# Four style-modulated convolution layers folded into one nine-tap convolution per sample: fifteen products of 512 columns, or twenty-four of 256 on even and odd columns

## The chip, the cores and the metric

The kernel runs on one core of one Trainium2 chip. The metric is device time in microseconds (us), the median of the runs shown; lower is better. The core's engines run side by side, each through its own list of instructions in the order written, and meet only at semaphores: TensorE (PE in the views; its weight loads are PEld), VectorE (DVE), ScalarE (ACT), GpSimd (POOL), and the queue engine SyncE (SP), which starts most of the DMA transfers.

## What is computed

128 samples of 64 channels and 1024 positions go through four 1D convolution layers with three taps each. The weights of a layer are scaled per sample by a style vector and normalised, and the input is added at the end:

```python
TYPES = ('same', 'upsample', 'same', 'downsample')
s = style @ mw.T + mb
weight = SCALE * w * s[:, None, :, None]
demod = lax.rsqrt(jnp.sum(weight * weight, axis=(2, 3)) + EPS)
weight = weight * demod[:, :, None, None]
# 'same': conv + bias; 'upsample': transposed conv, then blur [1,3,3,1];
# 'downsample': blur [1,3,3,1], then conv of stride 2
...
x = x + layers(x, cond_512)
```

Nothing nonlinear lies between the layers, so for one sample the chain is one convolution of nine taps, but for the outermost positions, which the kernel computes apart ("edges").

## The kernel before

**Layout.** A sample is 128 rows (two parities of the position times 64 channels) by 512 columns. In this form nine taps are five matrices of 128x128, one for each shift of a column. They are called W, and each sample has its own five.

**Groups and pairs.** Work goes by groups of NG = 4 samples (32 groups, for which weights are built) and by pairs of Q = 2 samples (loads, stores, splits of x). All in the program is float32, fed to TensorE as two parts of type fp32r: a high part (`xh`, `Wh`, made on ACT by a cast) and a low part (`xl`, `Wl`, the difference, made on DVE or POOL). A product is three matmuls, high by high, low by high, high by low (`split_mm`, L156 to L159).

**The main convolution** (`conv`) of a sample is five products with 512 columns, 15 matmuls, into one PSUM bank `po`. ACT then scales it, adds a bias and writes it to `T` (`t_out`, L398); POOL puts the edge values in (`finish`), and SP stores.

**The weights of a group** come out of seven units of TensorE, u0 to u6, each of which writes `pg`, one of three PSUM banks in rotation. Between them the results pass DVE (scaled by numbers per sample, `full`), ACT (high part, `high`) and POOL (low part, `low`):
- u0, u1 (10 matmuls): last two layers, result `Q2f`, high part `Q2h`, low parts `Q2l` and, for a lone half, `Q2h` written in place by POOL (L166).
- u2, u3 (24 matmuls) read Q2, result `Gf`, then `Gh`, `Gl`.
- u4, u5, u6 (22 matmuls) read G, result `Wf`; `ID`, made on POOL, adds the residual. `Wh` on ACT, `Wl` on DVE (`w_low`).
- `Q3f`, `Q3h`, `Q3l` feed u0 and u1, and are made three groups ahead.

Those are 56 matmuls of 256 columns for a group. SP then copies half of W across the partitions (`cross`, eight DMAs), since each matrix needs the blocks of two column shifts.

**The order** is written out by hand. Every engine loops over the samples b; i = b mod 4 is the slot in the group, and `SLOTS[i]` says which units, of how many groups ahead, TensorE runs ahead of conv(b), and the other engines go by the same table. In front of the loop a prologue makes the constants and the first weights.

```python
SLOTS = [[(1, 4), (2, 0), (2, 1)], [(1, 5), (1, 6)], [(2, 2)], [(2, 3)]]
for b in range(B):                       # TensorE
    for x in units_of(b):
        unit(*x)
    conv(b)
```

On DVE an iteration is: `x_low` for the pair after next (even b), then `full` for the slot's units, then `w_low` (slots 0 and 1), then a step of the edges (in four slots of group 0 and in slot 3 of groups 3 to 6, 11 to 14 and 19 to 22). On POOL it is: `ID` (slot 0), `low` of the slot's units, Q3 work (slots 2 and 3), `finish` (odd b).

Of the kernel before, what the change touches and what calls it, by code (L numbers as in the profile page):

```python
# [41 lines left out]
def build(nc, xin, xe, cw, a2, b1, q3, ed, wt, mwt, bb, st, eye, out):  # L42
    with ExitStack() as ctx:
# [96 lines left out]
        s_a2 = sem("a2l")  # L140
        s_pp, s_ch, s_one, s_ms, s_sq, s_sc, s_k0, s_b1 = (
            sem(n) for n in ("pp", "ch", "one", "ms", "sq", "sc", "k0", "b1"))


        SC_SQ2, SC_A2, SC_SQ, SC_A, SC_D, SC_K1, SC_K2, SC_K3, SC_CV = range(1, 10)

        K_A2, K_C, K_B1, K_B1D = 1, 2, 4, 8
# [41 lines left out]
        def _(sp):  # L189
            for n, dst, src in (("mwt", MW[:], mwt.rearrange("p (l m) -> p l m", l=4)),  # L190
                                ("bb", BB[:], bb.rearrange("p (k l) -> p k l", k=2)),
                                ("b1", b1w, b1),
                                ("q3", q3s[:], q3.rearrange("p (k o) -> p k o", k=2)),
                                ("eye", EYE[:], eye)):
# [49 lines left out]
        def _(pe):  # L244
            def conv(b):
                g, i = divmod(b, NG)
                n, q = divmod(b, Q)
# [4 lines left out]
                if q == 0:
                    pe.wait_ge(s_xh, n + 1)
                    pe.wait_ge(s_xl, n + 1)
                if b >= 2:
# [595 lines left out]
```

## Time and profile before

| | |
|---|---|
| median of 3 runs | 759.41 us (758.45 to 761.19) |
| the profiled execution | 762.67 us |
| its span, first to last instruction | 760.7 us |
| busy in the span: PE, DVE, ACT, POOL | 92%, 46%, 39%, 38% |
| TensorE's granted clock, mean | 0.984 |

Busy time adds up what an engine spent in instructions. A timeline row gives start, duration, engine, line of the kernel, operation, out<-in with shapes; brackets hold the idle time ahead of it and who ended it. The start-to-start distance of two matmuls is their real cost, since matmuls overlap. A windows row gives busy time of each engine in a stretch, then TensorE's granted clock, in which 1.00 is 2.4 GHz and 0.50 is 1.2 GHz.

### The profile page before, as it was taken

What the parts mean: (1) busy time and instruction counts of PE and PEld (TensorE: products, weight loads), DVE (VectorE), ACT (ScalarE), POOL (GpSimd) and SP (SyncE); (2) the same over time, 40 slices, a digit from 0 to 9 for tenths busy, and PEclk for the clock granted to TensorE, in tenths of its full rate; (3) what the DMA queues carried; (4) which work ended last, traced back from release to release, by engine and by line L of the source; (5) the groups of instructions that cost most, each with busy time, mean ns of one, the idle gap of its engine ahead of it and who ended that gap; (6) DMA issues with size and microseconds to landing.
All of it is one profiled execution on the core that took longest, in us unless ns stands there. A gap on an engine that the chain in (4) does not pass through costs nothing.

```text
span 760.7 us, 10551 instructions
## 1 busy us (share of the span) xinstructions
PE 702.8 (92%) x3830; PEld 608.2 (80%) x3830; DVE 348.7 (46%) x551; ACT 298.6 (39%) x435; POOL 289.3 (38%) x437
## 2 busy tenths in 40 slices
PE   2256989999999999999999999999999999999997
PEld 1245878888788888888888888888888888888886
DVE  5666663343555343443654433434654334334430
ACT  2222234444344444434344344443443444444432
POOL 5353134434333444334234444343334443433310
PEclk9986999999999999999999999999999999999999
DMA  7022455666766666666757766767657667667752
GB/s 251 0 42 77 92 138 124 152 162 131 161 156 159 161 144 147 157 148 145 168 144 155 162 143 155 151 144 170 154 134 168 147 152 156 144 161 174 174 145 84
DMA packets 187939, 109.00 MB, mean 143 GB/s; under 512 B 154032, under 2 KB 154288, under 8 KB 187888
## 3 DMA queue, kind: packets, MB, share of 16 engines
q1 hardware_dynamic: 187232, 106.56, 60.0%
q10 hardware_dynamic: 656, 1.77, 0.8%
q8 instruction: 31, 0.51, 0.3%
q14 instruction: 20, 0.16, 0.1%
HBM read 37.00 MB, written 33.55 MB: 93 GB/s over the span
## 4 chain that ended last, share of the span: by engine, by line
PE 73%; DVE 9%; POOL 8%; issue 6%; ACT 2%; DMA 1%; POOLq 0%; ACTq 0%; DVEq 0%
PE po L157 15%; PE po L158 15%; PE po L159 15%; PE pg L157 7%; PE pg L159 6%; PE pg L158 6%; PE pg L163 3%; PE pg L162 3%; DVE Gf L614 2%; POOL Q3h L166 2%; POOL Q3l L510 2%; POOL Gh L166 2%; POOL Gl L529 2%; ACT Gh L418 1%; DMA T<-in_wt 1%
## 5 line engine op out<-in xcount | busy, mean ns | idle before, releaser
L157 PE MATMUL po<-xh,Wh 128*128 128x512 f32 x640 | 253.5, 396 | 0.0
L159 PE MATMUL po<-xh,Wl 128*128 128x512 f32 x640 | 253.1, 396 | 0.0
L158 PE MATMUL po<-xl,Wh 128*128 128x512 f32 x640 | 253.0, 395 | 0.0
L398 ACT ACTIVATE T<-po,cv,DD 128x512 f32<-128x512 f32 x128 | 99.7, 779 | 155.7 <-PE po L159 155.5
L595 DVE TENSOR_TENSOR xl<-X,xh 128x1032 fp32r<-128x1032 f32 x64 | 81.8, 1278 | 142.8 <-ACT xh L391 142.6
L159 PEld LDWEIGHTS po<-xh,Wl 128*128 128x128 f32 x640 | 120.9, 189 | 28.2
L158 PEld LDWEIGHTS po<-xl,Wh 128*128 128x128 f32 x640 | 121.6, 190 | 23.3
L157 PEld LDWEIGHTS po<-xh,Wh 128*128 128x128 f32 x640 | 121.5, 190 | 23.1
L526 POOL TENSOR_TENSOR Gl<-Gf,Gh 128x512 fp32r<-128x512 f32 x32 | 41.5, 1297 | 231.4 <-ACT Gh L418 231.3
L423 ACT CAST Wh<-Wf 128x512 fp32r<-128x512 f32 x64 | 46.6, 727 | 153.9 <-DVE Wf L618 92.8
L518 POOL TENSOR_TENSOR Q2l<-Q2f,Q2h 128x512 fp32r<-128x512 f32 x32 | 44.1, 1377 | 121.4 <-ACT Q2h L413 121.4
L418 ACT CAST Gh<-Gf 128x512 fp32r<-128x512 f32 x64 | 39.7, 620 | 116.1 <-DVE Gf L614 116.1
L614 DVE TENSOR_TENSOR Gf<-pg,D10c 128x512 f32<-128x512 f32 x64 | 44.0, 688 | 85.3 <-PE pg L163 85.3
L391 ACT CAST xh<-X 128x1032 fp32r<-128x1032 f32 x64 | 66.7, 1042 | 6.6 <-DVE cv L769 6.6
L618 DVE TENSOR_TENSOR Wf<-pg,S 128x512 f32<-128x512 f32 x64 | 43.9, 686 | 53.5 <-PE pg L163 53.0
L630 DVE TENSOR_TENSOR Wl<-Wf,Wh 128x512 fp32r<-128x512 f32 x64 | 52.5, 820 | 30.2 <-ACT Wh L423 30.2
L157 PE MATMUL pg<-Q2h,B1h 128*128 128x256 f32 x192 | 56.3, 293 | 4.8 <-DVE B1dl L727 4.8
L157 PE MATMUL pg<-Gh,Ch 128*128 128x256 f32 x192 | 57.4, 299 | 3.0 <-DVE Wf L618 3.0
L159 PE MATMUL pg<-Q2h,B1l 128*128 128x256 f32 x192 | 55.8, 291 | 0.0
L158 PE MATMUL pg<-Q2l,B1h 128*128 128x256 f32 x192 | 55.7, 290 | 0.0
L159 PE MATMUL pg<-Gh,Cl 128*128 128x256 f32 x192 | 54.8, 285 | 0.0
L158 PE MATMUL pg<-Gl,Ch 128*128 128x256 f32 x192 | 54.7, 285 | 0.0
(155 smaller groups left out, 999.0 us busy)
## 6 DMA issues: line engine op xcount, KB each, us to landing
X<-in_xin SPq DMA_DIRECT2D x64, 516.0 KB, 5.9
out<-T SPq DMA_DIRECT2D x64, 512.0 KB, 3.6
Wh<-Wh SPq DMA_DIRECT2D x96, 128.0 KB, 2.9
Wl<-Wl SPq DMA_DIRECT2D x96, 128.0 KB, 3.2
Wh<-Wh SPq DMA_DIRECT2D x32, 192.0 KB, 4.9
Wl<-Wl SPq DMA_DIRECT2D x32, 192.0 KB, 5.3
E<-in_ed ACTq DMA_DIRECT2D x1, 768.0 KB, 9.8
XE<-in_xe SPq DMA_DIRECT2D x1, 576.0 KB, 11.8
```

What stands on the lines that cost most here:

```text
L157: eng.matmul(o, wh_, rh, start=first, stop=False)
L158: eng.matmul(o, wh_, rl, start=False, stop=False)
L159: return eng.matmul(o, wl_, rh, start=False, stop=last)
L391: act.copy(xh[:, n % XH], X[:, n % XR]).then_inc(s_xh, 1)
L398: act.activation(T[:, n % TR, b % Q], po[b % 2][:, :], ACT.Identity, bias=cv[:, b:b + 1], scale=DD[:, 3, b:b + 1]).then_inc(s_t, 1)
L418: act.copy(Gh[:, v], Gf[:, v]).then_inc(s_gh, 1)
L423: act.copy(wv(Wh, g, v), wv(Wf, g, v)).then_inc(s_wh, 1)
L518: pool.tensor_tensor(Q2l[:], Q2f[:, 0:2], r32(Q2h[:, 0:2]), ALU.subtract).then_inc(s_q2l, 1)
L595: tt(xl[:, n % XH], X[:, n % XR], r32(xh[:, n % XH]), ALU.subtract).then_inc(s_xl, 1)
L614: m = tt(v4(Gf[:, 2 * u - 4:2 * u - 2]), two, bc2(gs(D10c, g), 2, C), ALU.mult)
L618: m = tt(v4(Wf[:, 2 * u - 8:2 * u - 6]), two, bc2(gs(S[:, 0], g), 2, C), ALU.mult)
L630: tt(wv(Wl, g, v), wv(Wf, g, v), r32(wv(Wh, g, v)), ALU.subtract).then_inc(s_wl, 1)
```

## The change

The convolution of a sample is rewritten on even and odd columns. With W0 to W4 the five matrices, e the even and o the odd columns of x, both results share one sum: M[k] = (W0+W1) o[k] + (W2+W3) o[k+1] + W4 o[k+2]. The even result is M plus W0, W2, W4 applied to e-o, the odd one is M plus W1, W3 applied to the shifted e minus o. These are 3+3+2 products of 256 columns where five of 512 stood, so 24 matmuls of 256 columns, not 15 of 512.

For this
- POOL makes the two differences for each pair (`x_parts`, two operations of 128x516), in place in `X`; the row of `X`, `xh` and `xl` grows from 1032 to 1548 elements for a pair; the ring of `xh` and `xl` shrinks from three to two, that of `X` from four to three. `x_high` and `x_low` go one pair ahead, not two.
- POOL makes W0+W1, W2+W3 and W1+W2 (`sums`, 128x512 and 128x256), ACT and DVE their high and low parts (`sums_high`, `sums_low`).
- M has PSUM banks of its own (`pm`). ACT scales it and adds the bias (`m_out`, 128x256), and DVE adds it to both halves of `po` and writes `T` (`t_out`, 128x512, now on DVE, in front of the next sample's units).
- The weights lie with the four samples innermost, in one tensor `W`; a weight load of the convolution reads 128 columns that are 16 bytes apart. `cross` is five DMAs with runs of 256 elements, not 64.
- The slots change: u4, u5, u6 stand together in slot 0, u0 and u1 in slot 1.
- In the prologue DVE takes the low parts of group 0 and the running sums of `b1s` from POOL.

```diff
-SLOTS = [[(1, 4), (2, 0), (2, 1)], [(1, 5), (1, 6)], [(2, 2)], [(2, 3)]]
+SLOTS = [[(1, 4), (1, 5), (1, 6)], [(2, 0), (2, 1)], [(2, 2)], [(2, 3)]]
...
@@ TensorE, conv(b)
-                for j in range(5):
-                    w = [t[:, g % 2, j * NG + i].rearrange("p r o -> p (r o)") for t in (Wh, Wl)]
-                    m = split_mm(pe, po[b % 2][:, :], w[0], w[1], xh[:, n % XH, q, j:j + L2], xl[:, n % XH, q, j:j + L2],
-                                 j == 0, j == 4)
-                m.then_inc(s_o, 1)
+                def part(o, blocks, x):
+                    for j, v in enumerate(blocks):
+                        w = [W[:, g % 2, v, t].rearrange("p r (o b) -> p (r o) b", b=NG)[:, :, i] for t in range(2)]
+                        m = split_mm(pe, o, w[0], w[1], *[t[:, n % XH, q, x + j:x + j + 256] for t in (xh, xl)],
+                                     j == 0, j == len(blocks) - 1)
+                    return m
+                if b >= 2:
+                    pe.wait_ge(s_m, b - 1)
+                part(pm[b % 2], (5, 6, 4), HW).then_inc(s_mm, 1)
+                if b >= 2:
+                    pe.wait_ge(s_t, b - 1)
+                part(po[b % 2][:, 0:256], (0, 2, 4), 0)
+                part(po[b % 2][:, 256:512], (1, 3), 2 * HW).then_inc(s_o, 1)
...
@@ ACT
-            def t_out(b):
...
+            def m_out(b):
+                act.wait_ge(s_mm, b + 1)
+                if b >= 2:
+                    act.wait_ge(s_t, b - 1)
+                act.activation(M[:, b % 2, :], pm[b % 2], ACT.Identity,
+                               bias=cv[:, b:b + 1], scale=DD[:, 3, b:b + 1]).then_inc(s_m, 1)
+            def sums_high(g):
+                act.wait_ge(s_ws, 2 * g + 1)
+                act.copy(W[:, g % 2, 5:7, 0, 0], Wf[:, 5:7]).then_inc(s_wh, 1)
+                act.wait_ge(s_ws, 2 * g + 2)
...
+                act.copy(Wx[:, 0], Wf[:, 7]).then_inc(s_wh, 1)
...
@@ POOL
+            def x_parts(n):
+                pool.wait_ge(s_x[n % XR], 16 * (n // XR + 1))
+                x = X[:, n % XR]
+                pool.tensor_tensor(x[:, :, 2 * HW:3 * HW], x[:, :, 1:HW + 1], x[:, :, HW:2 * HW], ALU.subtract
+                                   ).then_inc(s_ab, 1)
+                pool.wait_ge(s_ab, 2 * n + 1)
+                pool.tensor_tensor(x[:, :, 0:HW], x[:, :, 0:HW], x[:, :, HW:2 * HW], ALU.subtract).then_inc(s_ab, 1)
...
+            def sums(g):
+                pool.wait_ge(s_ce, cnt(g, 5))
...
+                pool.tensor_tensor(Wf[:, 5:7], Wf[:, 0:4:2], Wf[:, 1:4:2], ALU.add).then_inc(s_ws, 1)
+                pool.tensor_tensor(Wf[:, 7], Wf[:, 1], Wf[:, 2], ALU.add).then_inc(s_ws, 1)
...
             for b in range(B):
                 g, i = divmod(b, NG)
                 if i == 0 and g + 1 < NGR:
                     identity(g + 1)
+                    sums(g + 1)
                 for x in units_of(b):
                     if x[1] < 4:
                         low(*x)
+                if b % Q == 0 and b and b // Q + 2 < NQ:
+                    x_parts(b // Q + 2)
...
@@ DVE
+            def t_out(b):
+                n, q = divmod(b, Q)
+                dve.wait_ge(s_m, b + 1)
+                dve.wait_ge(s_o, b + 1)
...
+                dve.scalar_tensor_tensor(out=T[:, n % TR, q].rearrange("p (e k) -> p e k", e=2),
+                                         in0=po[b % 2][:, :].rearrange("p (e k) -> p e k", e=2),
+                                         scalar=DD[:, 3, b:b + 1],
+                                         in1=M[:, b % 2, :].unsqueeze(1).to_broadcast([128, 2, 256]),
+                                         op0=ALU.mult, op1=ALU.add).then_inc(s_t, 1)
...
             for b in range(B):
                 g, i = divmod(b, NG)
-                if b % Q == 0 and b // Q + 2 < NQ:
-                    x_low(b // Q + 2)
+                if b:
+                    t_out(b - 1)
                 for x in units_of(b):
                     full(*x)
+                if b % Q == 0 and b and b // Q + 1 < NQ:
+                    x_low(b // Q + 1)
                 if i == 0 and g + 1 < NGR:
                     w_low(g + 1, 0)
-                if i == 1 and g + 1 < NGR:
                     w_low(g + 1, 1)
+                    sums_low(g + 1)
```

DVE in the main loop, from slot 0 of a group to its slot 2, before. `xl` is `x_low`, `Wf` are u4 to u6, `Q2f` u0 and u1, `Wl` `w_low`, `Gf` u2 or u3:

```order
L595 TENSOR_TENSOR xl<-X,xh 128x1032
L618 TENSOR_TENSOR Wf<-pg,S 128x512
L607 TENSOR_TENSOR Q2f<-pg,D 128x512
L609 TENSOR_TENSOR Q2f<-pg,D 128x256
L630 TENSOR_TENSOR Wl<-Wf,Wh 128x8x64
L618 TENSOR_TENSOR Wf<-pg,S 128x512
L622 TENSOR_TENSOR Wf<-Wf,ID 64x256
L624 TENSOR_TENSOR Wf<-pg,S 128x256
L630 TENSOR_TENSOR Wl<-Wf,Wh 128x12x64
L595 TENSOR_TENSOR xl<-X,xh 128x1032
```

The same engine and place after; here `W` and `Wx` are `w_low` and `sums_low`, and `T<-po,DD,M` is `t_out`:

```order
L665 TENSOR_TENSOR Wf<-pg,S 128x512 x2
L669 TENSOR_TENSOR Wf<-Wf,ID 64x256
L671 TENSOR_TENSOR Wf<-pg,S 128x256
L629 TENSOR_TENSOR xl<-X,xh 128x1548
L677 TENSOR_TENSOR W<-Wf,W 128x2x256
L677 TENSOR_TENSOR W<-Wf,W 128x3x256
L681 TENSOR_TENSOR W<-Wf,W 128x2x256
L683 TENSOR_TENSOR Wx<-Wf,Wx 64x256
L637 SCALAR_TENSOR_TENSOR T<-po,DD,M 128x512
L653 TENSOR_TENSOR Q2f<-pg,D 128x512
L655 TENSOR_TENSOR Q2f<-pg,D 128x256
```

The two operations on `Q2f` have moved from in front of all of the work on W to behind the whole of it, and five operations of two SBUF inputs now stand in a row between `Wf` and `t_out`.

POOL from slot 0 of a group to slot 1, before (`T<-EP` is `finish`):

```order
L537 TENSOR_TENSOR ID<-EYE,inv 128x256
L518 TENSOR_TENSOR Q2l<-Q2f,Q2h 128x512
L166 TENSOR_TENSOR Q2h<-Q2f,Q2h 64x256
L544 COPY T<-EP 128x2x2
L545 COPY T<-EP 128x2x2
```

The same engine and place after (`Wf<-Wf` is `sums`, `X<-X` `x_parts`):

```order
L558 TENSOR_TENSOR ID<-EYE,inv 128x256
L566 TENSOR_TENSOR Wf<-Wf 128x512
L567 TENSOR_TENSOR Wf<-Wf 128x256
L518 TENSOR_TENSOR X<-X 128x2x258
L521 TENSOR_TENSOR X<-X 128x2x258
L539 TENSOR_TENSOR Q2l<-Q2f,Q2h 128x512
L177 TENSOR_TENSOR Q2h<-Q2f,Q2h 64x256
```

`sums` and `x_parts` have come in between `ID` and the low parts of Q2.

## Rows read from the trace of the kernel before

**Rows 1.** The page: busy time, share of the span, instructions

```profile
PE 702.8 (92%) x3830; PEld 608.2 (80%) x3830; DVE 348.7 (46%) x551; ACT 298.6 (39%) x435; POOL 289.3 (38%) x437
```

**Rows 2.** Windows: stretch, length, busy PE, PEld, DVE, ACT, POOL, clock, DMA

```profile
145.52:255.05 109.53, 108.28 (x605) 94.01 (x605) 53.10 (x87) 45.40 (x66) 43.10 (x66) 1.00 0.67 151
642.71:663.81 21.10, 20.88 (x117) 18.05 (x117) 8.45 (x12) 9.12 (x14) 8.51 (x14) 1.00 0.70 157
```

**Rows 3.** Timeline of TensorE, steady: start, duration, line, operation

```profile
652.50 0.28 PE L157 MATMUL pg<-Q2h,B1h 128*128 128x256 f32 x1
...
654.05 0.28 PE L163 MATMUL pg<-Q2h,B1dl 128*128 128x256 f32 x1
654.17 0.39 PE L157 MATMUL po<-xh,Wh 128*128 128x512 f32 x1
...
654.87 0.39 PE L157 MATMUL po<-xh,Wh 128*128 128x512 f32 x1
```

**Rows 4.** Groups of VectorE by shape: busy us, mean ns, idle before

```profile
L595 DVE TENSOR_TENSOR xl<-X,xh 128x1032 fp32r<-128x1032 f32 x64 | 81.8, 1278 | 142.8 <-ACT xh L391 142.6
L630 DVE TENSOR_TENSOR Wl<-Wf,Wh 128x768 fp32r<-128x768 f32 x32 | 30.7, 958 | 28.8 <-ACT Wh L423 28.8
L630 DVE TENSOR_TENSOR Wl<-Wf,Wh 128x512 fp32r<-128x512 f32 x32 | 21.8, 681 | 1.4 <-ACT Wh L423 1.4
```

**Rows 5.** Groups of ScalarE by shape, same columns

```profile
L398 ACT ACTIVATE T<-po,cv,DD 128x512 f32<-128x512 f32 x128 | 99.7, 779 | 155.7 <-PE po L159 155.5
L418 ACT CAST Gh<-Gf 128x512 fp32r<-128x512 f32 x64 | 39.7, 620 | 116.1 <-DVE Gf L614 116.1
```

**Rows 6.** Groups of GpSimd by shape, same columns

```profile
L526 POOL TENSOR_TENSOR Gl<-Gf,Gh 128x512 fp32r<-128x512 f32 x32 | 41.5, 1297 | 231.4 <-ACT Gh L418 231.3
L505 POOL TENSOR_TENSOR Q3f<-q3s,D 128x512 f32<-128x512 f32 x31 | 32.6, 1051 | 0.2
L529 POOL TENSOR_TENSOR Gl<-Gf,Gh 128x256 fp32r<-128x256 f32 x32 | 23.7, 740 | 37.5 <-ACT Gh L418 37.5
```

**Rows 7.** Timeline of VectorE and of GpSimd where the two overlap

```profile
47.20 1.63 DVE L595 TENSOR_TENSOR xl<-X,xh 128x1032 fp32r<-128x1032 f32 x1
...
50.12 0.69 DVE L630 TENSOR_TENSOR Wl<-Wf,Wh 128x512 fp32r<-128x512 f32 x1 [0.69 <-ACT Wh L423]
50.73 0.68 DVE L618 TENSOR_TENSOR Wf<-pg,S 128x512 f32<-128x512 f32 x1
51.45 0.42 DVE L622 TENSOR_TENSOR Wf<-Wf,ID 64x256 f32<-64x256 f32 x1
51.79 0.41 DVE L624 TENSOR_TENSOR Wf<-pg,S 128x256 f32<-128x256 f32 x1
...
47.13 0.61 POOL L537 TENSOR_TENSOR ID<-EYE,inv 128x256 f32<-128x256 f32 x1
47.70 2.29 POOL L518 TENSOR_TENSOR Q2l<-Q2f,Q2h 128x512 fp32r<-128x512 f32 x1
50.14 1.26 POOL L166 TENSOR_TENSOR Q2h<-Q2f,Q2h 64x256 fp32r<-64x256 f32 x1
```

**Rows 8.** Windows of TensorE: stretch, length, busy PE, clock, DMA

```profile
40.70:44.35 3.65, 0.09 (x2) 1.00 0.00 0
44.35:47.90 3.55, 3.55 (x17) 0.53 0.00 0
...
99.10:101.79 2.69, 0.22 (x2) 1.00 0.00 0
...
102.60:105.90 3.30, 3.30 (x12) 0.50 0.48 158
```

**Rows 9.** Timeline of TensorE: first unit, first convolution, a unit in group 1's slot 0

```profile
28.00 0.55 PE L157 MATMUL pg<-Q3h,A2h 128*128 128x256 f32 x1 [8.70 <-POOL Q3h L166]
...
73.71 0.63 PE L157 MATMUL po<-xh,Wh 128*128 128x512 f32 x1
...
101.79 0.35 PE L157 MATMUL pg<-Q3h,A2h 128*128 128x256 f32 x1 [2.47 <-POOL Q3h L166]
```

More of the change, by code:

```diff
@@ L139, in build @@
         s_e, s_ed = sem("e"), sem("ed")
[L140 to L147, printed above, removed]
+        s_a2, s_cl = sem("a2l"), sem("cl")
+        s_pp, s_ch, s_one, s_ms, s_sq, s_sc, s_k0, s_b1, s_bs = (
+            sem(n) for n in ("pp", "ch", "one", "ms", "sq", "sc", "k0", "b1", "bs"))
+        SC_SQ2, SC_A2, SC_SQ, SC_D32, SC_A, SC_D, SC_K1, SC_K2, SC_K3, SC_CV = range(1, 11)
+        K_A2, K_C, K_B1, K_B1D = 1, 2, 3, 4
         r32 = lambda ap: ap.bitcast(F32)
@@ L345, in _ @@
             for l in range(4):
-                m = pe.matmul(ps[:, l * 128:l * 128 + 128], MW[:, l, :], ST[:, :], start=True, stop=True)
+                m = pe.matmul(ps[:, l * 128:l * 128 + 128], MW[:, l, :], ST, start=True, stop=True)
             m.then_inc(s_pp, 1)
@@ L427, in _ @@
             act.wait_ge(s_in["wt"], 16)
+            act.activation(SQ[:, 2], WT[:, 2], ACT.Square).then_inc(s_sq, 1)
             act.activation(SQ[:, 0:2], WT[:, 0:2], ACT.Square)
@@ L472, in _ @@
                         high(*x)
+                m_out(b)
+                if i == 0 and g + 1 < NGR:
+                    sums_high(g + 1)
                 if i == 3 and g + 3 < NGR:
                     q3_high(g + 3)
-            t_out(B - 1)
         @block.gpsimd
@@ L558, in _ @@
             low(1, 1)
+            sums(0)
             q3_full(2)
@@ L562, in _ @@
             low(1, 3)
+            x_parts(1)
+            x_parts(2)
             for b in range(B):
@@ L719, in _ @@
             reached(dve.tensor_scalar(AA[:, 3], psv[:, 3], EPS, None, ALU.add))
+            dve.wait_ge(s_k0, K_B1)
+            tt(B1l[:, :, 0, :], b1s[:, 0:11:2, :], r32(B1h[:, :, 0, :]), ALU.subtract)
+            tt(B1l[:, :, 1, :], b1s[:, 2:13:2, :], r32(B1h[:, :, 1, :]), ALU.subtract).then_inc(s_b1, 1)
             full(0, 0)
@@ L734, in _ @@
             full(0, 2)
+            full(0, 3)
+            dve.wait_ge(s_gh, 1)
+            tt(Gl[:, 0:2], Gf[:, 0:2], r32(Gh[:, 0:2]), ALU.subtract).then_inc(s_gl, 1)
+            dve.wait_ge(s_gh, 2)
+            tt(Gl[:, 2], Gf[:, 2], r32(Gh[:, 2]), ALU.subtract).then_inc(s_gl, 1)
+            lone_low(dve, Gh[hi, 3, :], Gf[hi, 3, :]).then_inc(s_gl, 1)
+            link(dve.reciprocal(RR[:, 3], RR[:, 3]))
             newton(slice(3, 4))
             reached(tt(inv3[:], AA[:, 3], DD[:, 3], ALU.mult))
-            full(0, 3)
             full(1, 0)
             full(1, 1)
-            x_low(0)
             full(0, 4)
-            w_low(0, 0)
             full(0, 5)
             full(0, 6)
+            w_low(0, 0)
             w_low(0, 1)
+            x_low(0)
+            sums_low(0)
             dve.wait_ge(s_in["ed"], 16)
@@ L787, in _ @@
                         edge_in(c + 1)
+            t_out(B - 1)
 def layouts(x, cond_512, w, bia, mw, mb):
```

298 lines of the change are left out of this document (156 added, 142 removed).

## The prediction, made before the changed kernel ran

> **What bounds the kernel now.** I read the page first: TensorE is busy 92% of the span, no other engine half of it [rows 1]. Then the windows: one group of four samples takes 21.10 us [rows 2]. The timeline gives the price of a matmul in it as the distance of two starts: 13 distances of 256 columns take 1.55 us, 0.119 each; three of 512 take 0.70 us, 0.233 each [rows 3]. So 56 unit matmuls (6.7) and 60 convolution matmuls (14.0) are 20.7 us; 0.4 us of the 21.1 is waiting. TensorE is the bound, and the other engines have slack: DVE 8.45 busy in 21.10, POOL 8.51 [rows 2].
>
> **What TensorE saves.** 96 matmuls of 256 columns at 0.119 are 11.4 us where 60 of 512 took 14.0. TensorE's work in a group falls to 18.1 us. Were it still the bound, 31 groups would give back some 90 us. I argue that it isn't: the change puts work and order on DVE and POOL that close a longer loop.
>
> **Durations of what is new.** For each the nearest row, ends behind it.
> - `x_low`, 1548 elements: the undelayed 1032 take 1.23 (1.63 less a delay worked out below [rows 7]) and 512 take 0.68 [rows 4]. That is 1.06 ns for an element, so 1.78 us (1.7 to 1.9).
> - `t_out` on DVE: as another 512 out of PSUM, 0.68 [rows 7]; up to 0.78, which ACT took [rows 5]. `w_low` 0.68 and 0.96 [rows 4], `sums_low` 0.68 and 0.42 [rows 4, 7].
> - `m_out` on ACT, 256: 0.40 to 0.78, taken 0.56; it frees ACT and lies beside other work [rows 5].
> - POOL: `x_parts` 1.30 twice a pair (1.05 to 1.40), `sums` 1.30 and 0.74 [rows 6]. POOL gets 7.2 us a group on top of its 8.5, DVE 4.9 on top of its 8.45 (`t_out` 2.7, `xl` 1.1, `sums_low` 1.1).
> - Series on DVE step by duration less 0.08: 50.73, then 51.45 behind a semaphore, 51.79 [rows 7].
>
> **Two inputs in SBUF on DVE and a read on POOL don't run together.** At 47.13 POOL's `ID` starts (0.61, ends 47.74); `xl` starts at 47.20 and ends 48.83; `Q2l` on POOL starts at 47.70 and ends 49.99, for 2.29 instead of 1.3. Each time the second ends at the first one's end plus its own duration less 0.15: 47.74+1.23-0.15 = 48.82; 48.83+1.30-0.15 = 49.98. It holds for `Wl` and `Q2h` too: 50.81+0.74-0.15 = 51.40, the row's 50.14+1.26. `Wf` out of PSUM, begun at 50.73 beside the same `Q2h`, took its plain 0.68, so one SBUF input doesn't collide, and `t_out` won't [rows 7]. The Trainium skill, "SBUF — State Buffer", section "Who interferes with whom", has the same collision, but as a lock for the whole instruction. By it each of the seven turns below would cost 0.15 us more, a group 1.1 us; the rows' 0.15 of overlap stands in my sum.
>
> **The new loop, u2 of one group to u2 of the next.** Before, u0 and u1 ran in slot 0 and u2 in slot 2, two convolutions later. Now u0 and u1 are in slot 1, and between them and u2 stands one convolution (24 x 0.119 = 2.9 us), while DVE does all work on W ahead of `full` of u0. First with no collision and no idle engine:
> - TensorE from u2 to the end of u5: u2 14, conv 24, u3 10, conv 24, u4 9, u5 11, which is 92 matmuls, 10.95 us, and 0.2 until DVE sees it.
> - DVE: u5 0.68, `ID` added 0.50, u6 0.35, `x_low` 1.70, `w_low` 0.60 and 0.88, `sums_low` 0.60 and 0.35, `t_out` 0.60, `full` of u0 0.68: 6.9 us.
> - ACT 0.65, POOL 1.30 for `Q2l`, 0.08, 0.74 for the lone half, 0.1 to TensorE: 2.9 us.
>
> That is 21.0 us, more than TensorE's 18.1 and no less than the group of before. The loop alone eats the gain.
>
> Now with POOL's turns, t = 0 at u2's start. TensorE has waited before u2, so I take its clock as low at first: after 2.7 and 3.65 us of idle it ran at 0.50 for some 3.4 us, 0.21 for a matmul of 256 [rows 8]. u2 ends at 3.0, its Gf at 3.9, Gh at 4.55. DVE goes on with `x_low` from 3.8 to 5.6, so POOL's `Gl` ends at 6.75, `x_parts` at 9.4, `Q3f` at 10.4. u3's low halves, ready to start at 9.5, run 10.45 to 11.95. u4 ended at about 12.0, so u5 starts at 12.05 and ends 13.35. POOL: two Q3 halves 13.55, `finish` 13.9, `ID` 14.5. DVE adds `ID` by 14.95. From there both engines take turns, each with the step above: `sums` a to 16.3, `x_low` 17.9, `sums` b 18.5, `w_low` a 19.05, `x_parts` a 20.2, `w_low` b 21.0, `x_parts` b 22.15, `sums_low` a 22.7, b 23.05. `t_out` 23.65, `full` of u0 24.25, Q2h 24.9, Q2l 26.25, lone half 27.05, u2 at **27.1 us**. TensorE ended the convolution of slot 1 at 20.5 and idles 6.6 us.
>
> **The sum.** Before the first convolution DVE makes u0's Q3 parts at once, not behind 2 us of `B1l` on POOL; I take 67 us for 73.7 (65 to 74). Group 0, with four steps of the edges, was 28.1 us [rows 9]; it was 7 over a plain group, and I take 10 over the new one, 37. Groups 1 to 29 have a u2 ahead: 29 x 27.1 = 786. In groups with an edge step DVE was busy (53.10 - 5 x 8.45)/4 = 2.7 us more each, and the group grew by only (109.53 - 5 x 21.10)/4 = 1.0 [rows 2]. In the new loop DVE's step comes ahead of u5's `full` after a wait for TensorE: 3.3 each, 12 x 3.3 = 40. The last two groups have no u2: 16 (their W chain) and 12; the tail 4. 67+37+786+40+16+12+4 = 962 us of span. The profiled execution is 2 over its span and 3 over the median, so I say **960 us**, 26% slower. Cross copies (fewer, longer runs) and the rings of two and three cost nothing: W is ready some 9 us before its convolution, and `xh` frees a slot early.
>
> **The rivals.**
> 1. *The same turns, but the clock stays high.* u2 then ends 1.3 us earlier and so does POOL's chain: 25.8 a group, 38 less: 920.
> 2. *The turns cost little* (DVE and POOL slip into each other's gaps, or `x_parts` reads in another way). The loop of 21.0 with POOL's u3 halves is 21.3, with the clock low after a wait of 3 us 22.6. 67+34+29x21.3+30+28+4 = 781, up to 818: 800. Against it: the steps of [rows 7] fit to 0.01 us.
> 3. *Strided weight loads.* No row has a weight load with columns 16 bytes apart. Below, it costs nothing; above, the step of 0.119 hides at least a whole load now [rows 3], and a load of twice that would make a convolution matmul 0.238. The loop holds 48 of them, 5.7 us, of which 1 hides behind POOL: 29 x 4.7 = 136, so 1096. The Trainium skill, "SBUF — State Buffer", the note on cachelines, says that each access to a new line of 16 bytes pays a penalty, and that two hits in a line are needed for full bandwidth; that would bring this rival, though the same note calls a stride of 4 fp32 free. By the first reading 1096, by the second 960.
> 4. *TensorE remains the bound* (the other side). The loop must then lose 3 us more than the rows allow, say by DVE's subtractions on the new layout going at twice the speed, or by waits of u2 that I place wrongly. Then 67 + 28 + 29 x 18.4 + 30 + 4 + 12 = 675. It decides at a loop of 18.1, and faster than before begins at one of about 20.
> 5. *A loop of 20 to 20.5*: no change.
>
> **Chances.** Forecast 0.43, rival 1 0.15, rival 2 0.14, rival 3 0.13, rival 4 0.12, rival 5 0.03. Forecast and rivals 1 to 3 are 0.85, so the range reaches from 775 to 1110; the forecast's own is 900 to 1010. A measurement of this kernel tells 0.3% from no change: faster 0.12, same 0.03, slower 0.85.
>
> **What would show it.** A group of 27 us in the windows, with TensorE idle in one piece before u2 (`Q2h, B1h`), released by POOL's lone half of Q2; TensorE some 67% busy; its clock at 0.50 after that idle time; POOL's `sums` and `x_parts` and DVE's `xl` and `W` stretched far over their plain durations, in turns; DVE's stretch from u5 to `t_out` 8 us long. Wrong, if u2 follows the convolution of slot 1 at once, if those durations stay plain (rival 2), if the matmuls on `W` step by more than 0.13 in warm stretches (rival 3), or if the first convolution is not before 74 us.

## The result, and the profile after

The changed kernel takes **1092.79 us** (1091.89 to 1093.98), the kernel before 759.45 (758.45 to 761.19): 1.439 times as long, interval 1.4357 to 1.4417. That is inside the forecast's wide range, but 133 us over its value, and within 3 us of what the third rival gave (1096).

The page of after, as [rows 1] for before, and two of its groups (busy us, mean ns, idle before):

```profile
PE 988.9 (91%) x4982; PEld 979.1 (90%) x4982; DVE 561.3 (51%) x755; ACT 334.3 (31%) x498; POOL 607.7 (56%) x615
...
L566 POOL TENSOR_TENSOR Wf<-Wf 128x512 f32<-128x512 f32 x32 | 140.2, 4381 | 145.3 <-DVE Wf L669 145.3
...
L168 PEld LDWEIGHTS po<-xh,W 128*128 128x128 f32 x640 | 211.8, 331 | 0.0
```

TensorE is as busy as before, 91%, though its matmuls go over fewer columns in all. The windows, columns as in [rows 2], show one plain group:

```profile
611.38:641.86 30.48, 29.39 (x152) 29.23 (x152) 15.09 (x19) 10.28 (x16) 19.14 (x20) 1.00 0.49 126
```

A group is 30.48 us, not 21.10, at the full clock, and TensorE fills 29.39 of it with 152 matmuls. The timeline of TensorE at the end of slot 1, as [rows 3], tells why:

```profile
639.35 0.40 PE L170 MATMUL po<-xh,W 128*128 128x256 f32 x1
...
640.75 0.39 PE L170 MATMUL po<-xh,W 128*128 128x256 f32 x1
642.23 0.35 PE L168 MATMUL pg<-Q2h,B1h 128*128 128x256 f32 x1 [1.08 <-POOL Q2h L177]
642.42 0.28 PE L169 MATMUL pg<-Q2l,B1h 128*128 128x256 f32 x1
642.54 0.28 PE L170 MATMUL pg<-Q2h,B1l 128*128 128x256 f32 x1
642.65 0.28 PE L168 MATMUL pg<-Q2h,B1h 128*128 128x256 f32 x1
```

Six distances of the convolution's 256 columns take 1.40 us, 0.233 each, as much as 512 columns took [rows 3]; those of a unit take 0.12 as ever. So 96 x 0.2335 + 56 x 0.119 = 29.1, and some 1.3 us of waiting ahead of u2 make the group. The convolution costs 22.4 us a group where the old one cost 14.0.

Behind that the forecast's loop is there too. DVE and GpSimd from u5's `Wf` to u2's low parts:

```profile
629.24 0.42 DVE L669 TENSOR_TENSOR Wf<-Wf,ID 64x256 f32<-64x256 f32 x1
629.58 0.41 DVE L671 TENSOR_TENSOR Wf<-pg,S 128x256 f32<-128x256 f32 x1
629.91 1.75 DVE L629 TENSOR_TENSOR xl<-X,xh 128x1548 fp32r<-128x1548 f32 x1
631.59 1.54 DVE L677 TENSOR_TENSOR W<-Wf,W 128x512 fp32r<-128x512 f32 x2
634.96 1.62 DVE L681 TENSOR_TENSOR W<-Wf,W 128x512 fp32r<-128x512 f32 x1 [1.82 <-ACT W L441]
636.61 1.21 DVE L683 TENSOR_TENSOR Wx<-Wf,Wx 64x256 fp32r<-64x256 f32 x1
637.85 0.75 DVE L637 SCALAR_TENSOR_TENSOR T<-po,DD,M 128x512 f32<-128x512 f32 x1
...
629.73 4.54 POOL L566 TENSOR_TENSOR Wf<-Wf 128x512 f32<-128x512 f32 x1 [3.42 <-DVE Wf L669]
634.23 0.74 POOL L567 TENSOR_TENSOR Wf<-Wf 128x256 f32<-128x256 f32 x1
634.94 1.10 POOL L518 TENSOR_TENSOR X<-X 128x516 f32<-128x516 f32 x1
636.11 1.43 POOL L521 TENSOR_TENSOR X<-X 128x516 f32<-128x516 f32 x1
639.93 1.28 POOL L539 TENSOR_TENSOR Q2l<-Q2f,Q2h 128x512 fp32r<-128x512 f32 x1 [2.39 <-ACT Q2h L427]
641.35 0.73 POOL L177 TENSOR_TENSOR Q2h<-Q2f,Q2h 64x256 fp32r<-64x256 f32 x1
```

From the start of DVE's `ID` operation (629.24) to u2 (642.23) it takes 13.0 us, where the prediction had 12.6 (14.5 to 27.1). TensorE is busy with the slow convolution through nearly all of it and idle for 1.1 us.

### The profile page after: what moved, and what is told of

The parts are those of the page before. It is cut to its first block, busy times and chain, and to the rows that moved or that the text cites. A ratio compares the mean times of both kernels' runs of the same rounds, so it can differ in the third digit from the quotient of the medians.

```text
span 1090.6 us, 13458 instructions
## 1 busy us (share of the span) xinstructions
PE 988.9 (91%) x4982; PEld 979.1 (90%) x4982; DVE 561.3 (51%) x755; ACT 334.3 (31%) x498; POOL 607.7 (56%) x615
## 4 chain that ended last, share of the span: by engine, by line
PE 49%; POOL 19%; DVE 19%; issue 8%; ACT 4%; DVEq 0%; DMA 0%; POOLq 0%; SPq 0%
POOL Wf L566 13%; PE po L168 7%; PE po L170 7%; PE po L169 7%; PE pg L168 5%; PE pm L169 4%; PE pm L170 4%; PE pm L168 4%; PE pg L170 4%; PE pg L169 4%; POOL Q2l L539 3%; DVE Wx L683 3%; DVE T L637 3%; DVE Wf L665 3%; POOL Q2h L177 2%
## 5 line engine op out<-in xcount | busy, mean ns | idle before, releaser
L168 PE MATMUL po<-xh,W 128*128 128x256 f32 x640 | 254.7, 398 | 0.0
L169 PE MATMUL po<-xl,W 128*128 128x256 f32 x640 | 254.7, 398 | 0.0
L170 PE MATMUL po<-xh,W 128*128 128x256 f32 x640 | 254.1, 397 | 0.0
L566 POOL TENSOR_TENSOR Wf<-Wf 128x512 f32<-128x512 f32 x32 | 140.2, 4381 | 145.3 <-DVE Wf L669 145.3
L169 PEld LDWEIGHTS po<-xl,W 128*128 128x128 f32 x640 | 211.9, 331 | 0.0
L168 PEld LDWEIGHTS po<-xh,W 128*128 128x128 f32 x640 | 211.8, 331 | 0.0
L170 PEld LDWEIGHTS po<-xh,W 128*128 128x128 f32 x640 | 211.7, 331 | 0.0
L169 PE MATMUL pm<-xl,W 128*128 128x256 f32 x384 | 153.5, 400 | 0.0
L170 PE MATMUL pm<-xh,W 128*128 128x256 f32 x384 | 153.4, 399 | 0.0
L168 PE MATMUL pm<-xh,W 128*128 128x256 f32 x384 | 152.4, 397 | 0.0
L169 PEld LDWEIGHTS pm<-xl,W 128*128 128x128 f32 x384 | 127.0, 331 | 0.0
L170 PEld LDWEIGHTS pm<-xh,W 128*128 128x128 f32 x384 | 126.9, 331 | 0.0
L168 PEld LDWEIGHTS pm<-xh,W 128*128 128x128 f32 x384 | 124.7, 325 | 0.0
L629 DVE TENSOR_TENSOR xl<-X,xh 128x1548 fp32r<-128x1548 f32 x64 | 113.5, 1774 | 6.1 <-ACT xh L406 6.1
```

What stands on the lines that cost most here:

```text
L168: eng.matmul(o, wh_, rh, start=first, stop=False)
L169: eng.matmul(o, wh_, rl, start=False, stop=False)
L170: return eng.matmul(o, wl_, rh, start=False, stop=last)
L566: pool.tensor_tensor(Wf[:, 5:7], Wf[:, 0:4:2], Wf[:, 1:4:2], ALU.add).then_inc(s_ws, 1)
L629: tt(xl[:, n % XH], X[:, n % XR], r32(xh[:, n % XH]), ALU.subtract).then_inc(s_xl, 1)
```

## The experiments

Theory: the weight load's stride sets the convolution's step (the distance of two starts), and without it the prediction's walk through a group holds. Rival: something else in the 256-column products, or in the reads of x, makes them slow.

**c1: neighbouring weights.** Only the address of the convolution's weight loads differs; the products then use the wrong columns of `W`.

```diff
-w = [W[:, g % 2, v, t].rearrange("p r (o b) -> p (r o) b", b=NG)[:, :, i] for t in range(2)]
+w = [W[:, g % 2, v, t].rearrange("p r n -> p (r n)")[:, 128 * i:128 * i + 128] for t in range(2)]
```

> The changed kernel with one thing different: a weight load of the convolution reads 128 neighbouring elements and not 128 that are 16 bytes apart. It therefore multiplies by wrong weights; all else, every instruction and wait, is as in the changed kernel. Theory L (the strided load sets the step of the convolution's matmuls, 0.2335 us in the changed kernel): the step falls to 0.119, TensorE's own work in a group falls from 29.1 to 18.1 us, and the group of 30.5 us becomes the loop through DVE and POOL that the prediction works out, 26 to 27.1 us with a low clock after the idle time: 950 to 990 us in all. If that loop is weaker than worked out: group 21.5 to 24, 800 to 880 us. Rival M (the step comes from something else in the new matmuls, such as the shifted moving columns or the PSUM halves): step stays 0.2335, 1093 us. Rival of a TensorE that is the bound again: group 18.4, 675 us.

Measured 974.6 us (974.07 to 975.5), ratio 1.2824 (1.2795 to 1.2853). Windows of a group, of TensorE's wait and of the stretch behind it, and TensorE's timeline at the end of the wait:

```profile
605.14:632.52 27.38, 20.80 (x152) 20.63 (x152) 15.11 (x18) 10.04 (x16) 19.09 (x20) 0.87 0.55 140
625.85:632.52 6.67, 0.45 (x4) 0.24 (x2) 5.03 (x6) 2.85 (x5) 4.05 (x4) 0.91 0.00 0
632.52:635.90 3.38, 3.03 (x14) 3.06 (x15) 0.00 (x0) 0.13 (x1) 0.52 (x3) 0.50 0.56 187
...
632.87 0.55 PE L168 MATMUL pg<-Q2h,B1h 128*128 128x256 f32 x1 [6.57 <-POOL Q2h L177]
```

The step is 0.119 us, and this is the kernel that the prediction described: a group of 27.34 us (27.1 foretold), TensorE idle for 6.6 us ahead of u2 behind GpSimd's lone half of Q2 (6.6 foretold), then 3.4 us at half the clock, and 974.6 in all (960). The load's addresses alone make the 118 us between c1 and after.

**c2, c3, b4: which stride.** c2 takes every second column of `W` (8 bytes apart), c3 every third (12), again wrong ones; b4 is the kernel before with its loads 16 bytes apart.

```diff
c2 +...rearrange("p r n -> p (r n)")[:, 64 * i:64 * i + 256:2]
c3 +...rearrange("p r n -> p (r n)")[:, 32 * i:32 * i + 382:3]
b4 -w = [t[:, g % 2, j * NG + i].rearrange("p r o -> p (r o)") for t in (Wh, Wl)]
b4 +w = [t[:, g % 2, j * NG:(j + 1) * NG].rearrange("p n r o -> p (n r o)")[:, i:512:4] for t in (Wh, Wl)]
```

> As c1_contiguous, but the weight load's elements are 8 bytes apart (wrong weights again). If a load costs more only from 16 bytes on, or as soon as two elements share a line of 16 bytes it is free: step 0.119 and the time of c1_contiguous within 1%. If the cost grows with the distance: load between 190 and 331 ns, step about 0.16 to 0.18, group 27 to 29.

> As c1_contiguous, with elements 12 bytes apart (wrong weights again), so that three of four elements open a new line of 16 bytes. If the limit is a distance of 16 bytes: as c1_contiguous. If each new line costs: the step is near 0.2, time near that of the changed kernel, 1050 to 1093 us.

> The kernel before with one thing different: the weight load of the 512-column matmuls reads 128 elements 16 bytes apart (wrong weights). Theory L with a load that runs beside the matmul ahead (step is the longer of the two): the load needs 0.2335, the matmul 0.233, so the step and the 759 us stay within 1%, and the load's duration rises from 190 to 331 ns. If load and matmul share the time in part (0.233 plus the extra 0.115), the step is 0.35, a group 21.1 + 60 x 0.115 = 28.0 and the time 970 to 985 us. If strides cost nothing (rival M): 759 us and loads of 190 ns.

Measured c2 975.05, c3 1028.17 (one run each), b4 780.12 us (779.82 to 781.1; ratio 1.0263, 1.0236 to 1.029). c2 came out as its first case. c3 lies between its two cases, and b4 above the 1% of its theory. The weight loads of the first product in the groups by shape, of c1, c2, c3 (mean 196, 202, 264 ns; 331 in after, above), then of before and of b4:

```profile
L168 PEld LDWEIGHTS po<-xh,W 128*128 128x128 f32 x640 | 125.5, 196 | 3.3 <-DVE T L637 3.3
```

```profile
L168 PEld LDWEIGHTS po<-xh,W 128*128 128x128 f32 x640 | 129.1, 202 | 3.3 <-DVE T L637 3.3
```

```profile
L168 PEld LDWEIGHTS po<-xh,W 128*128 128x128 f32 x640 | 169.2, 264 | 0.2 <-DVE T L637 0.2
```

```profile
L157 PEld LDWEIGHTS po<-xh,Wh 128*128 128x128 f32 x640 | 121.5, 190 | 23.1
```

```profile
L157 PEld LDWEIGHTS po<-xh,Wh 128*128 128x128 f32 x640 | 198.6, 310 | 0.2
```

TensorE's timelines at the full clock, of c2, c3 and then b4:

```profile
597.58 0.28 PE L168 MATMUL po<-xh,W 128*128 128x256 f32 x1
...
599.16 0.28 PE L169 MATMUL po<-xl,W 128*128 128x256 f32 x1
```

```profile
600.05 0.34 PE L168 MATMUL po<-xh,W 128*128 128x256 f32 x1
...
600.91 0.34 PE L170 MATMUL po<-xh,W 128*128 128x256 f32 x1
```

```profile
599.93 0.40 PE L158 MATMUL po<-xl,Wh 128*128 128x512 f32 x1
...
601.60 0.40 PE L159 MATMUL po<-xh,Wl 128*128 128x512 f32 x1
```

Thirteen steps of c2 take 1.58 us, 0.121 each. Five of c3 take 0.86, 0.172 each (over all convolutions of the trace the median is 0.1745). Seven of b4 take 1.67, 0.239 each. So with loads 4, 8, 12 and 16 bytes apart a product of 256 columns steps by 0.119, 0.121, 0.1745 and 0.234 us. The last two are 128 x 12 and 128 x 16 bytes at 8.8 bytes per ns, an estimate from two points; at 8 bytes it gives 0.116, less than the product's own step, so the runs can't tell whether a load at 8 bytes is dearer than one at 4.

In b4 the same slow load lies beside 512 columns of 0.233, and it costs 20 us in all, where the halved product pays 118. That fits a load that runs beside the product, with the longer of the two setting the step. It fits but for 0.005 us a step in b4 (a median of 0.238, with 0.233 before), some 10 of its 20 us; where the other 10 went stays open.

The Trainium skill, "SBUF — State Buffer", in its note on cachelines, asks for two hits in a line of 16 bytes and calls a stride of 4 fp32 free. The runs agree with the first as far as they show it (at 8 bytes the step is 0.121, not 0.119) and not with the second (at 16 bytes the step doubles). Whether the load pays for distance or for each line of 16 bytes that it touches, they can't tell: the number of such lines, 96 at 12 bytes and 128 at 16, grows as the distance does, and both come to 1.8 ns a line.

**c5: the clock.** c1 with 40 products of constants ahead of u2, into a bank that no one reads then.

```diff
+                if b % NG == 2 and b > NG:
+                    last = max((5 * c + k + 2 for (gg, ii), (c, k) in edge_at.items() if NG * gg + ii < b), default=0)
+                    pe.wait_ge(s_ed, last)
+                    for _ in range(40):
+                        pe.matmul(pe_[:, 0:256], A2h[:, 0:128], A2h[:, 0:256], start=True, stop=True)
```

> c1_contiguous with 40 matmuls of constants (256 columns, 4.8 us at the high clock) put into TensorE's idle 6.85 us ahead of u2; they write a free bank and nothing reads it. In c1_contiguous a group is 27.3 us, 6.8 of it at the low clock. If the low clock after the idle time is part of the loop: clock 1.00 throughout, the group falls by 1.3 to 1.9 us to 25.4 to 26.0 us, 915 to 935 us in all, in spite of 40 matmuls more a group. If the clock costs nothing because DVE and POOL set the loop: 975 us as c1_contiguous. If TensorE were the bound, the group would grow by 4.8 us.

Measured 944.49 us (one run), above the 915 to 935 of its theory; a group in the windows:

```profile
597.07:622.96 25.89, 23.66 (x194) 23.14 (x194) 15.11 (x18) 9.83 (x15) 19.09 (x20) 1.00 0.58 148
```

In this group the clock stays at 1.00 and the time falls by 1.45 us to 25.89, where the prediction's first rival put it (25.8). Over groups 1 to 29 the gain is 32 us, 1.1 a group: in 12 of the 29 TensorE now stands for 0.3 us or more (up to 1.4) ahead of slot 0's convolution, where c1 has no wait at all. What it waits for there stays open.

**c6: GpSimd's new work.** c1 with `x_parts` and `sums` of the main loop cut to one or two columns.

```diff
+                e = HW if n < XR else 1
-                pool.tensor_tensor(x[:, :, 0:HW], x[:, :, 0:HW], x[:, :, HW:2 * HW], ALU.subtract).then_inc(s_ab, 1)
+                pool.tensor_tensor(x[:, :, 0:e], x[:, :, 0:e], x[:, :, HW:HW + e], ALU.subtract).then_inc(s_ab, 1)
...
+                e = NC if g == 0 else 2
+                pool.tensor_tensor(Wf[:, 5:7, 0:e], Wf[:, 0:4:2, 0:e], Wf[:, 1:4:2, 0:e], ALU.add).then_inc(s_ws, 1)
```

> c1_contiguous with the work that the change put on POOL taken out (its four x_parts and two sums of a group work on one or two columns only; the convolution gets stale parts), all waits as before. Theory T (turns: a DVE operation with two SBUF inputs and a POOL operation that reads exclude each other, and the sums wait behind xl and W): ID to u2 falls from 12.6 to about 8.4 us, the group from 27.3 to 22.5 to 23.6 us, 830 to 860 us in all. If POOL's operations cost the loop only by their own length where they stand on it: x_parts stand beside DVE's work, and only the first sums (1.3) and a part of the rest goes: group 25.5 or more, 915 us or more. If the loop is DVE's alone: 975 us.

Measured 867.29 us (one run), a group of 23.68, both just above its theory and far from its rivals: GpSimd's added work is 3.7 us of c1's group. That even the little that is left of it waits is in the timeline, DVE first, then GpSimd:

```profile
582.32 0.42 DVE L671 TENSOR_TENSOR Wf<-Wf,ID 64x256 f32<-64x256 f32 x1
582.66 0.41 DVE L673 TENSOR_TENSOR Wf<-pg,S 128x256 f32<-128x256 f32 x1
582.99 1.75 DVE L631 TENSOR_TENSOR xl<-X,xh 128x1548 fp32r<-128x1548 f32 x1
584.67 1.54 DVE L679 TENSOR_TENSOR W<-Wf,W 128x512 fp32r<-128x512 f32 x2
...
582.81 3.47 POOL L568 TENSOR_TENSOR Wf<-Wf 128x4 f32<-128x4 f32 x1 [2.03 <-DVE Wf L671]
586.23 0.19 POOL L569 TENSOR_TENSOR Wf<-Wf 128x2 f32<-128x2 f32 x1
```

Four elements a partition took 3.47 us; two took 0.19. The first ended at 586.28, 0.07 us behind DVE's series of three operations (584.67 + 1.54 = 586.21).

**d1: samples outermost again.** The 24 products with `W` = [128, 2, 2, 7 x 4, 2, 64] and ten cross copies with runs of 64 elements, all of it computed.

```diff
-w = [W[:, g % 2, v, t].rearrange("p r (o b) -> p (r o) b", b=NG)[:, :, i] for t in range(2)]
+w = [W[:, g % 2, t, v * NG + i].rearrange("p r o -> p (r o)") for t in range(2)]
```

> The change without its layout: the 24 products, sums, x_parts and slots of the changed kernel, but the weights with the samples outermost as in the kernel before (each load reads 128 neighbouring elements; the cross copies have runs of 64 elements and are ten, not five). It computes the reference. If the layout's only price is the strided load: 975 us within 1%, as c1_contiguous. If the short runs of the cross copies come late: group over 28 us, TensorE waits ahead of the convolution of slot 0 and not of u2, 1000 us or more.

Measured 977.35 us (976.57 to 979.05), ratio 1.2851 (1.2828 to 1.2875), a plain group of 27.4 as in c1, within 3 us of c1 in all. The layout costs nothing but its load.

**d2: the order.** d1 with u0 and u1 back in slot 0, ahead of DVE's work on W.

```diff
-SLOTS = [[(1, 4), (1, 5), (1, 6)], [(2, 0), (2, 1)], [(2, 2)], [(2, 3)]]
+SLOTS = [[(1, 4), (1, 5), (1, 6), (2, 0), (2, 1)], [], [(2, 2)], [(2, 3)]]
```

> d1_samples_outer with u0 and u1 back in slot 0, behind u4 to u6; it computes the reference. Theory S (it is the slot of u0 and u1, behind DVE's work on W, that closes the loop): TensorE no longer waits 6.8 us ahead of u2, clock 1.00 in plain groups; what bounds next is POOL, whose 15.3 us a group and DVE's 5.6 us with two SBUF inputs exclude each other: group 20 to 21.5 us, 730 to 790 us in all. If POOL's exclusion doesn't bind: 18.2 to 18.6, 670 to 700 us. If the slot doesn't matter: 975 us.

Measured 814.16 us (808.12 to 817.01), ratio 1.0715 (1.0689 to 1.0742), above the 730 to 790 of its theory; a group of 21.7 to 21.9. The order was worth 163 us: the long loop is the second cause. What TensorE still waits for, from its timeline:

```profile
306.86 0.36 PE L168 MATMUL pg<-Gh,Ch 128*128 128x256 f32 x1 [1.50 <-POOL Gh L177]
309.85 0.39 PE L173 MATMUL pg<-Q3h,A2h 128*128 128x256 f32 x1 [0.18 <-DVE Wf L676]
311.55 0.35 PE L168 MATMUL pm<-xh,W 128*128 128x256 f32 x1 [1.20 <-ACT W L443]
```

**d3, d4: GpSimd's chain and the copies.** d3 is d2 with `x_parts` on DVE in slots 1 and 3, d4 also issues the first cross copies ahead of a store.

```diff
d3 @@ DVE, main loop, behind full
+                if b % Q == 1 and b > Q and b // Q + 2 < NQ:
+                    x_parts(b // Q + 2)
d4 @@ SP
+                if g + 1 < NGR:
+                    cross(g + 1, 0)
                 if n:
                     store(n - 1)
                 if g + 1 < NGR:
-                    cross(g + 1, 0)
                     cross(g + 1, 1)
```

> The last kernel (samples outermost in the weights, u0 and u1 in slot 0) with x_parts of the main loop on DVE instead of GpSimd, in slots 1 and 3, two differences for each pair. The whole result is computed. Theory (GpSimd's chain and the reads that exclude each other set the group): GpSimd loses 4.4 us a group of plain work, the low parts of G follow at once and the wait of 1.8 us between u4 and u5 goes; two-input work in SBUF on DVE and GpSimd adds up to 9.0 and 10.0 us a group, 17 with the overlaps, under TensorE's 18.1. DVE's plain work rises from some 12 to 14.7 us. A group of 19.5 to 20.5 us, 745 to 775 us in all. Rival (DVE becomes the bound): DVE stands ahead of TensorE in every slot, and what GpSimd gains DVE loses; the group stays within 0.5 us of 21.7, 800 to 820 us.

> As the run before it, and the first six cross copies of a group are issued ahead of the store of the pair before, not behind it. The whole result is computed. In the kernel with u0 and u1 in slot 0 the queue waited with them for the store from 294.2 us, when W's low parts were done, to 298.3, and TensorE stood 1.4 us ahead of slot 0's convolution. Theory (that wait is the last copy's landing): it goes, 1.4 us a group less where nothing else is late next, and a group of 18.5 to 19.5 us, 715 to 745 us. Rival (the wait is DVE's, which frees the PSUM banks late): no change against the run before, within 3 us.

Measured d3 777.32 us (776.35 to 777.95; ratio 1.022, 1.019 to 1.0251), d4 774.55 (772.59 to 775.61; 1.0184, 1.0155 to 1.0212). d3 gained 37 us and ended 2 us above the range of its theory. DVE and GpSimd still took turns in it, one for one (DVE first, then GpSimd):

```profile
281.83 1.81 DVE L641 TENSOR_TENSOR xl<-X,xh 128x1548 fp32r<-128x1548 f32 x1
283.56 3.17 DVE L689 TENSOR_TENSOR W<-Wf,W 128x512 fp32r<-128x512 f32 x2
...
281.96 2.26 POOL L574 TENSOR_TENSOR Wf<-Wf 128x256 f32<-128x256 f32 x1
284.19 1.72 POOL L546 TENSOR_TENSOR Q2l<-Q2f,Q2h 128x512 fp32r<-128x512 f32 x1
```

d4 gave 3 us and not 30; that is its rival's number, but with another cause: in d3 the wait ahead of slot 0's convolution was gone in most groups already. The store waits for GpSimd's `finish`, and with `x_parts` off GpSimd the copies were issued 1.8 us behind W's low parts (286.73 to 288.56), where d2 had 4.1 (294.2 to 298.3). So the price that d4 was to win had been won by d3. A plain group of d4:

```profile
277.36:298.05 20.69, 19.02 (x152) 18.44 (x152) 18.95 (x23) 9.68 (x16) 15.07 (x16) 1.00 0.83 190
```

That is 0.4 us less than before [rows 2], with DVE busy 18.95 of 20.69.

**d5, d6: two more orders.** d5 is d4 with the steps of the edges in slot 1 (TensorE's part ahead of its convolution) and GpSimd's Q3f behind the low parts of u3; d6 is d5 with Q3f, its high and low halves and `ID` in slot 1.

```diff
d5 -                edge_at[(EC // NG * c - 5 + k, 3)] = (c, k)
d5 +                edge_at[(EC // NG * c - 5 + k, 1)] = (c, k)
d6 @@ POOL, main loop, behind finish
+                if i == 1 and g + 3 < NGR:
+                    q3_full(g + 3)
+                if i == 1 and g + 2 < NGR:
+                    identity(g + 2)
+                if i == 1 and g + 3 < NGR:
+                    q3_low(g + 3)
```

> The last kernel with two moves in the order: in groups past the first the steps of the edges run in slot 1, which has no units, with TensorE's part ahead of its convolution, not behind slot 3; and GpSimd's Q3f comes behind the low parts of u3, not ahead of them. The whole result is computed. Theory (what still holds the time above that of before is DVE's edge step of some 5 us ahead of u4's full, and GpSimd's Q3f ahead of the lone half that u5 waits for): in the last kernel a plain group took 20.7 us with 1.27 us between u4 and u5, and the four groups of a chunk of edges 11 us more than plain ones. About 7 us of each chunk go, 20 in all, and 0.8 us in each of some 29 groups: 730 to 750 us, faster than before by 1 to 4 per cent. Rival (DVE, busy 88%, is full): only its idle time of 1.6 us a group can be won, and an edge step costs the same wherever it stands; 755 to 770 us.

> The last kernel, with GpSimd's Q3f, its low halves and ID (and ScalarE's Q3h) for the next groups in slot 1, where GpSimd had nothing to do for 4.5 us, and not in slots 2, 3 and 0. The whole result is computed. In the last kernel Q3f behind the low parts of u3 made u0 wait 1.9 us for Q3's lone half and left 0.8 us ahead of u5: GpSimd's chain through ScalarE was only turned round. Theory (that chain is all that stretches slot 0): of the 20.7 us of a plain group in the kernel before the last, the 1.27 us between u4 and u5 fall to at most 0.8, the 0.47 us between u0 and u1 go, and nothing waits for Q3; a group of 19.4 to 20.2 us, 725 to 755 us. Rival (DVE is full, its stretched work on W decides): the group stays at 20.5 to 20.7 us, and only the edges give something, 765 to 772 us.

Measured d5 803.85 us (802.28 to 804.22; ratio 1.0568, 1.0549 to 1.0588), d6 774.96 (774.4 to 775.53; 1.019, 1.0164 to 1.0216). Both are outside their theory and their rival: d5 was to take 730 to 750 or 755 to 770, d6 725 to 755 or 765 to 772. For d5, GpSimd and TensorE show why:

```profile
304.70 1.04 POOL L537 TENSOR_TENSOR Q3f<-q3s,D 128x512 f32<-128x512 f32 x1
306.47 0.72 POOL L541 TENSOR_TENSOR Q3l<-Q3f,Q3h 128x256 fp32r<-128x256 f32 x1 [0.73 <-ACT Q3h L428]
307.27 0.73 POOL L177 TENSOR_TENSOR Q3h<-Q3f,Q3h 64x256 fp32r<-64x256 f32 x1
...
308.15 0.36 PE L168 MATMUL pg<-Q3h,A2h 128*128 128x256 f32 x1 [1.59 <-POOL Q3h L177]
```

Q3f has a way through ScalarE and back before u0 can start; moved back by one place it came late by 1.6 us, and a group took 22.0. d6 takes it from there, and a plain group falls to 20.37:

```profile
267.28:287.65 20.37, 18.93 (x154) 18.37 (x153) 18.12 (x23) 9.79 (x15) 15.76 (x16) 1.00 0.83 189
```

Yet the time stays at 775. Both d4 and d6 beat the old kernel in a plain group and lose in the others: the four groups with a step of the edges (and the one behind them) cost 11 to 15 us more than plain ones for each of three chunks, where the old kernel paid 4 x 1.0 [rows 2]. None of these versions beats 759 us.

## Why the prediction missed its value and kept its side

Its terms against the two runs, from the starts of the first convolution matmul of groups 0, 1 and 30 in TensorE's timeline:

| term of the sum, us | predicted | c1 | after |
|---|---|---|---|
| up to the first convolution | 67 | 72.0 | 71.5 |
| group 0 | 37 | 28.9 | 34.3 |
| 29 groups, each | 27.1 | 27.34 | 30.48 |
| 29 groups | 786 | 792.9 | 883.9 |
| edges (in the runs: all that groups 1 to 29 took beyond plain ones) | 40 | 39.4 | 51.3 |
| last two groups and tail | 32 | 39.3 | 49.6 |
| span | 962 | 972.6 | 1090.6 |

The range held because it took in the third rival, at a chance of 0.13; the value of 960 was 133 us off.

1. **The walk was right.** With the load made plain (c1), its group, its idle time, the length of the low clock and the sum of the edges come out within 1 to 2%, and the releaser is the one it named. The edges do so in sum only: 3.3 us were foretold for each of the four groups of a chunk, and c1's groups 3 to 7 took 0.9, 0.6, 6.1, 2.9 and 2.1 more than plain ones. u0 and u1 behind DVE's work on W close a loop that TensorE can't fill (d2 took 163 us of it back), and the reads that exclude each other stretch it (c6, 3.7 us a group; a part of that is GpSimd's plain work).
2. **The step that failed is the price of the strided weight load.** No row showed one, and the forecast took the lower bound, nothing, with a chance of 0.13 for the upper. The upper came out within 2%: a step of 0.234 (0.238 foretold), 118 us in all between c1 and after. A hint was there: 608.2 us of loads by 3830 [rows 1] are 0.159 each, more than the 0.119 between two starts [rows 3], so no row showed slack for a longer load at 256 columns. It was no more than a hint, for c1 has records of 196 ns at the same step of 0.119, and its load does not set that step: c2's, with elements twice as far apart, adds 0.002.
3. **The third rival's group was 31.8 and is 30.48**, because it added 4.7 us to a group that still held 1.3 us of low clock. With TensorE idle for 1.1 us instead of 6.6 the clock stays at 1.00 (the window of 611.38): 31.8 - 1.3 = 30.5. That is 38 us less in 29 groups, and prologue, group 0, edges and tail gave 31 of it back. So 1093 against 1096 is luck to that extent.
4. **Who goes first was wrong, the sum right.** The prediction let DVE and GpSimd alternate, beginning with `sums`. In after `sums` starts at 629.73, waits for `xl` and both parts of W, ends at 634.27 (DVE's end at 633.13 + 1.30 - 0.15 = 634.28) and takes 4.54 us; then ScalarE and `sums_low` wait for it. The rule of the ends holds; the order does not. It cost the walk nothing in sum: DVE ended its series with `Wx` 8.6 us behind the start of `ID` (637.82), where the prediction had 8.55 (14.5 to 23.05). The 13.0 us instead of 12.6 arose behind it, in 4.4 us from there to u2 instead of 4.05.
5. **Smaller terms.** `x_parts` takes 1.10, not 1.30; `xl` 1.75 (1.78 foretold), `t_out` 0.75 (0.68). The first unit starts at 20.1 instead of 28.0 [rows 9], but the first convolution only 2.2 us earlier: before it TensorE stood 10.3 us (to 50.1) and 8.4 us (to 66.5) behind a chain of small operations on DVE (`tmp`). Group 0 was 8 us cheaper than its guess; the two last groups and the tail 7 dearer in c1.
6. **The new minimum.** In d6 TensorE's work is 18.1 us of 20.37, and DVE is busy for 18.12 of it. That the fourth rival, TensorE as the bound, would need a lighter DVE first is argued from this; no run took work off DVE in that order.

## What to carry to other kernels

Where an edit shortens the products, ask what their length had hidden: the strided weight load cost 2.6% beside products of 512 columns and 12% beside products of 256. Where no row shows an operand's pattern, price it by the bound that the kernel is nearest to, or try that one address by itself, as c1 did. And before counting what fewer products give back, walk the loop that the new order closes.

## What the runs showed of the hardware that was not expected

- Beside a product of 256 columns a weight load of 128 columns (fp32r) costs nearly the same with elements 4 and 8 bytes apart (a step of 0.119 and 0.121 us) and more beyond: 0.1745 at 12, 0.234 at 16 bytes, an estimated 8.8 bytes per ns.
- GpSimd's operation that reads SBUF can come out behind a whole series of DVE's operations with two SBUF inputs, and not behind one: 4.54 us for 1.30 of work in after (the same in 30 of its groups), 3.47 for four elements in c6. It had started 0.18 us ahead of `xl`, and `xl` took its plain 1.75. It isn't the series alone that does it. In d3 (and in most groups of d2 and d6) the same series stood without a gap, but there GpSimd's operation started 0.13 us behind `xl`: it ended behind `xl` alone (281.83 + 1.81 + 0.74 - 0.15 = 284.23; the row's 281.96 + 2.26), and DVE's two operations on W took 3.17 us, not 1.54. And in [rows 7] GpSimd's `ID`, 0.07 us ahead, did delay `xl`. The Trainium skill, "SBUF — State Buffer", section "Who interferes with whom", says that whoever issues first has the shared ports for the whole instruction; [rows 7] and d3 agree, and the starts of after and c6 don't. What decides stays open.
- A wait of 6.6 us cost more than itself, by the clock's 3.4 us at 0.50 behind it: 1.45 us in the group shown, 1.1 us a group over the run (c1 against c5). Behind the 1.1 us of idle time in after the clock stayed at 1.00.
